# A post-norm decoder layer on one core: inner layer transposed by DMA, its maxima in PSUM, row sums taken with the residual, and new orders on all engines

## The reference

```python
x = _layernorm(x + _L0_attn_ref(x))          # itself x + message; per position l: softmax(q q^T / 8) q over 32 x 64
x = _layernorm(x + _L0_xattn_ref(x, ctx_4096, ctx_4096, ...))
x = _layernorm(x + _L0_ffn_ref(x, ...))

# cross attention, 8 heads of 64, per batch (linear attention):
qh = softmax(Wq x, axis=-2) * SCALE; kh = softmax(Wk ctx, axis=-1); vh = Wv ctx
context = einsum('bhdn,bhen->bhde', kh, vh); out = einsum('bhde,bhdn->bhen', context, qh)
out = Wo out + bo; out / max(|out|, 1e-12) * g * 8

# inner layer, 512 -> 1376 -> 512:
mx_linear(silu(mx_linear(x, w_gate)) * mx_linear(x, w_up), w_down)
# mx_linear quantizes both operands: in each group of 32 along the last axis,
# scale = 2^(floor(log2(max|x|)) - 7), then rounding to an 8-bit float, times scale
```

## Time and profile before

| | us |
|---|---|
| median of 3 runs (725.84 to 727.15) | 726.65 |
| the profiled execution | 726.31 |
| its span in the profile | 724.5 |
| busy in it: PE, DVE, POOL, ACT | 659.2, 601.4, 504.5, 459.7 |
| mean granted TensorE clock, share of full | 0.964 |

### The profile page before, as it was taken

The page is one execution under the profiler, slowest core; times in us unless marked ns, Lnnn a source line. Parts: engine busy times, 40 slices in busy tenths (PEclk is TensorE's granted clock), DMA queues, the critical chain, the costliest instruction groups (busy, mean ns, idle before and its releaser), DMA issues.

```text
span 724.5 us, 14262 instructions
## 1 busy us (share of the span) xinstructions
PE 659.2 (91%) x5392; PEld 361.2 (50%) x5392; DVE 601.4 (83%) x897; ACT 459.7 (63%) x837; POOL 504.5 (70%) x631
## 2 busy tenths in 40 slices
PE   0649898899999999999999999999999989898894
PEld 0649895344454454454554454444545544454451
DVE  2749967997978999998898988888986479989995
ACT  3319574887686787787687787677776523444353
POOL 1512735887888688788878878688777567735785
PEclk9956999999999999999999999999999999999998
DMA  8990002010001010010110110110100000111102
GB/s 311 162 246 8 31 31 67 14 24 0 30 9 31 7 38 29 8 38 1 37 38 1 37 38 2 37 30 4 42 8 12 8 16 16 43 45 52 44 29 88
DMA packets 38916, 31.07 MB, mean 43 GB/s; under 512 B 21184, under 2 KB 29376, under 8 KB 38848
## 3 DMA queue, kind: packets, MB, share of 16 engines
q1 hardware_dynamic: 38848, 30.16, 15.5%
HBM read 21.82 MB, written 4.19 MB: 36 GB/s over the span
## 4 chain that ended last, share of the span: by engine, by line
PE 70%; DVE 13%; issue 7%; POOL 5%; ACT 2%; DMA 2%; SPq 0%; POOLq 0%; DVEq 0%; ACTq 0%
PE banks L2461 9%; PE banks L2471 9%; PE banks L2508 8%; PE banks L2428 8%; PE banks L2438 8%; PE banks L2485 8%; PE banks L2545 5%; PE banks L2413 4%; PE banks L2396 3%; DVE big L876 2%; DMA big<-in_x_dram 2%; PE banks L2523 2%; PE banks L2515 2%; DVE big L881 2%; DVE big L1039 1%
## 5 line engine op out<-in xcount | busy, mean ns | idle before, releaser
L1659 ACT ACTIVATE big<-banks 128x512 f32<-128x512 f32 (+1 forms) x336 | 188.6, 592 | 103.5 <-PE banks L2461 47.7
L548 POOL TENSOR_TENSOR big<-big 128x512 f32<-128x512 f32 x128 | 134.6, 1064 | 10.8 <-DVE big L981 10.8
L1720 ACT ACTIVATE big<-banks,big 128x512 f32<-128x512 f32 x128 | 87.3, 687 | 22.2 <-DVE big L961 22.1
L961 DVE TENSOR_REDUCE big<-banks 128x1 f32<-128x512 f32 x128 | 82.1, 675 | 15.4 <-PE banks L2428 15.4
L540 POOL TENSOR_TENSOR big<-big 128x512 f32<-128x512 f32 x64 | 84.5, 1328 | 11.1 <-ACT big L1725 11.1
L2461 PEld LDWEIGHTS banks<-ident,big 128*128 128x128 f32 x512 | 55.3, 142 | 68.3 <-issue 46.3
L967 DVE TENSOR_REDUCE big<-banks 128x16 f32<-128x1024 f32 x64 | 77.2, 1206 | 14.0 <-PE banks L2438 13.7
L2471 PEld LDWEIGHTS banks<-ident,big 128*128 128x128 f32 x512 | 54.7, 141 | 64.9 <-ACT big L1659 38.6
L2461 PE MATMUL banks<-ident,big 128*128 128x128 f32 x512 | 81.6, 284 | 1.1 <-ACT big L1659 0.9
L972 DVE TENSOR_TENSOR big<-banks,big 128x1024 f32<-128x1024 f32 x64 | 77.8, 1215 | 3.4 <-PE banks L2471 2.1
L2471 PE MATMUL banks<-ident,big 128*128 128x128 f32 x512 | 77.6, 282 | 1.0 <-ACT big L1659 0.7
(11 more groups left out here) (104 smaller groups left out, 1188.9 us busy)
## 6 DMA issues: line engine op xcount, KB each, us to landing
big<-in_x_dram SPq DMA_DIRECT2D x8, 1024.0 KB, 13.9
big<-in_ctx_dram SPq DMA_DIRECT2D x16, 256.0 KB, 3.0
out_dram<-big SPq DMA_DIRECT2D x16, 256.0 KB, 2.1
big<-in_L_ffn_w_down_dram SPq DMA_DIRECT2D x4, 688.0 KB, 10.1
big<-in_L_ffn_w_gate_dram SPq DMA_DIRECT2D x10, 256.0 KB, 2.6
big<-in_L_ffn_w_up_dram SPq DMA_DIRECT2D x10, 256.0 KB, 2.7
wg_area<-in_L_xattn_Wq_dram SPq DMA_DIRECT2D x2, 128.0 KB, 11.1
wg_area<-in_L_xattn_Wk_dram SPq DMA_DIRECT2D x2, 128.0 KB, 6.8
```

What stands on the lines that cost most here:

```text
L548: pool.tensor_tensor(e, e, r, ALU.mult).then_inc(s.p_ready, 1)
L1659: return act.activation(dst, src, ACT.Copy)
L1720: act.activation(EK[:, f % 2, par, i], bank[par], ACT.Exp, bias=kneg[:, par, i:i + 1], accum_out=ksum[:, f % 2, par, i:i + 1]).then_inc(s. ...
```

## The change

Four parts. (1) `transpose_h` moves from TensorE and ACT to SP: two DMA transposes for each tile, of 6 and 5 blocks, straight from `hq` to `hqT`, with their own semaphores; `hq` gets 32 zero columns more, cleared once by POOL. (2) In `scale_hidden` the maxima lie in PSUM (banks 4 and 5, free by then); DVE also computes the scale and keeps it there, and `dequant_hidden` reads it there. (3) `add_down` adds the residual and sums each row in one instruction; POOL makes the mean (`out_mean`), ACT squares the centred row and sums it (`square_out`), and `out_stats` is gone. (4) All orders behind the self-attention are written out anew, call by call, without loops, with a new table for `tr_no`, and SP's queue too.

```diff
+            def transpose_h(u, r):
+                sp.wait_ge(s.hq_ready, u + 1)
+                if u < 2:
+                    sp.wait_ge(s.hq_cleared, 1)
+                else:
+                    sp.wait_ge(s.down_part, 2 * u + r - 3)
+                f0, f1 = ((0, 6), (6, FT))[r]
+                sp.dma_start_transpose(hqT[:, u % 2, f0:f1], hq[:, u % 2, P * f0:P * f1]
+                                       ).then_inc(s.h_transposed[2 * (u % 2) + r], 16)
...
+            def out_mean(u):
+                k = u % 2
+                pool.wait_ge(s.down_added, u + 1)
+                pool.tensor_scalar(neg_mean_o[:, k:k + 1], sum_o[:, k:k + 1], -1.0 / L, None, ALU.mult
+                                   ).then_inc(s.out_mean_ready, 1)
...
-                group_max(hk[u % 2][0], hs[:, u % 4]).then_inc(s.h_inv_ready, 1)
+                else:
+                    dve.wait_ge(s.tr_copied, len(tr_no))
+                amax = bank[4 + u % 2][:, 0:GH]
+                ch.link(dve.tensor_reduce(amax, groups(hs[:, u % 4]), X, ALU.max, apply_absolute_value=True))
+                ch.link(dve.tensor_scalar(hk[u % 2][0].bitcast(I32), amax.bitcast(I32), 0x7F800000, None, ALU.bitwise_and))
+                dve.tensor_scalar(amax, hk[u % 2][0], TINY, 2.0 ** -7, ALU.max, ALU.mult).then_inc(s.h_inv_ready, 1)
...
-                dve.tensor_tensor(groups(hq[:, u % 2]), groups(h8), spread(hk[u % 2][2], GH), ALU.mult
+                dve.tensor_tensor(groups(hq[:, u % 2, 0:FFN]), groups(h8), spread(bank[4 + u % 2][:, 0:GH], GH), ALU.mult
                                   ).then_inc(s.hq_ready, 1)
...
-                dve.tensor_tensor(yo[:, u % 2], xt[:, u], bank[6 + u % 2], ALU.add).then_inc(s.down_added, 1)
-
-            def out_stats(u):
...
+                dve.tensor_tensor_reduce(out=yo[:, u % 2], in0=xt[:, u], in1=bank[6 + u % 2], scale=1.0, scalar=0.0,
+                                         op0=ALU.add, op1=ALU.add, accum_out=sum_o[:, u % 2:u % 2 + 1]
+                                         ).then_inc(s.down_added, 1)
...
+            def square_out(u):
+                k = u % 2
+                act.wait_ge(s.out_mean_ready, u + 1)
...
+                act.activation(spare, yo[:, k], ACT.Square, bias=neg_mean_o[:, k:k + 1],
+                               accum_out=square_o[:, k:k + 1]).then_inc(s.out_squared, 1)
...
             def down(u, r):
-                pe.wait_ge(s.tr_copied, tr_no[u, f"h{r}"] + 1)
+                pe.wait_ge(s.h_transposed[2 * (u % 2) + r], 16 * (u // 2) + 16)
```

More of the change, by code:

```diff
@@ L288, in decoder_kernel @@
         s.hq_ready = sem("hq_ready")
+        s.hq_cleared = sem("hq_cleared")
+        s.h_transposed = [sem(f"h_transposed_{part}") for part in range(4)]
         s.down_part = sem("down_part")
         s.down_added = sem("down_added")
+        s.out_mean_ready = sem("out_mean_ready")
+        s.out_squared = sem("out_squared")
         s.out_ready = sem("out_ready")
@@ L367, in decoder_kernel @@
-        for t, group in middle_groups:
-            tr_no[t, group] = len(tr_no)
-        for u in range(7, 9):
-            for behind, group in turn_groups:
-                if u - behind in tiles:
-                    tr_no[u - behind, group] = len(tr_no)
-        for t, group in last_groups:
-            tr_no[t, group] = len(tr_no)
+        transposed = (
[36 rows of a table added]
+        )
+        tr_no = {group: n for n, group in enumerate(transposed)}
         def aw_group(a):
@@ new lines, in _ @@
+            load_aw(0)
+            load_item(0)
+            load_item(1)
+            load_x(0)
+            load_x(1)
+            load_x(2)
+            load_x(3)
+            load_small()
+            load_xq(0)
+            load_xq(1)
+            load_xq(2)
+            load_xq(3)
+            load_aw(1)
+            load_aw(2)
+            load_item(2)
+            load_aw(3)
+            load_ctx(0)
+            load_ctx(1)
+            transpose_item(0)
+            load_aw(4)
+            load_aw(5)
@@ new lines, in _ @@
+            transpose_h(3, 1)
+            transpose_h(4, 0)
+            transpose_x(9)
+            store(0)
+            transpose_h(4, 1)
+            transpose_h(5, 0)
+            transpose_h(5, 1)
+            store(1)
+            transpose_x(10)
+            store(2)
+            transpose_x(11)
+            transpose_h(6, 0)
+            store(3)
+            transpose_h(6, 1)
+            transpose_h(7, 0)
+            transpose_h(7, 1)
+            transpose_x(12)
+            transpose_x(13)
@@ new lines, in _ @@
+            transpose_h(8, 0)
+            transpose_h(8, 1)
+            store(4)
+            transpose_h(9, 0)
+            transpose_h(9, 1)
+            store(5)
+            transpose_x(14)
+            store(6)
+            transpose_x(15)
+            transpose_h(10, 0)
+            transpose_h(10, 1)
+            transpose_h(11, 0)
+            store(7)
+            transpose_h(11, 1)
+            transpose_h(12, 0)
+            transpose_h(12, 1)
+            transpose_h(13, 0)
+            store(8)
@@ L463, in _ @@
+            store(9)
+            transpose_h(13, 1)
+            store(10)
+            transpose_h(14, 0)
+            transpose_h(14, 1)
+            store(11)
+            transpose_h(15, 0)
+            transpose_h(15, 1)
+            store(12)
+            store(13)
+            store(14)
+            store(15)
             for slot in range(2):
@@ L591, in _ @@
             shift_aw(0)
[L592 removed]
             shift_item(0)
[L594 to L597 removed]
+            for n in range(0, 5):
+                norm_scores(n)
             shift_aw(1)
@@ L2333, in _ @@
+            silu(14, 1)
+            square_out(9)
+            silu(14, 2)
+            result(8)
+            result(9)
+            silu(15, 0)
+            silu(15, 1)
+            silu(15, 2)
+            square_out(10)
+            square_out(11)
+            result(10)
+            result(11)
+            square_out(12)
+            for n in range(13, 16):
+                square_out(n)
+                result(n - 1)
+            result(15)
         @block.tensor
@@ L3038, in _ @@
-            transpose_h(T - 2, 1)
-            down(T - 2, 0)
-            down(T - 2, 1)
-            transpose_h(T - 1, 0)
-            transpose_h(T - 1, 1)
-            down(T - 1, 0)
-            down(T - 1, 1)
+            gate_up(14, 1)
+            gate_up(14, 2)
+            down(10, 0)
+            down(10, 1)
+            gate_up(15, 0)
+            gate_up(15, 1)
+            down(11, 0)
+            down(11, 1)
+            gate_up(15, 2)
+            for n in range(12, 16):
+                down(n, 0)
+                down(n, 1)
```

3263 lines of the change are left out of this document (1858 added, 1405 removed), and 46 rows, old and new, of tables (first_groups, transposed).

## The result

The changed kernel takes 689.96 us (median of 4, 688.46 to 691.75) where the kernel before takes 726.25 in the same series: ratio 0.950, 95% interval 0.947 to 0.953. A second series, on another occasion, gave 0.948 (0.946 to 0.950). The forecast was 692.3, with a range from 680 to 711. The profiled execution took 688.46 us with a span of 686.7, against 726.31 and 724.5.

The account below looks back on a forecast made before the run. TensorE was taken to bound the attention alone, TensorE and DVE together the inner layer. 726.3 - 7.6 (transposes) - 17.9 (attention order) - 9.5 (inner layer) + 1.0 (tail) = 692.3 us, range 680 to 711.

Parts of the forecast that it names:

- h off TensorE: Tiles outside the tail: removing 12.5 transposes of h, 0.61 us each, from TensorE saves 7.6 us.
- the inner layer's loss: Inner layer: 11.45 us of idle TensorE and 2.5 us of lowered clock, 14 us, of which 9.5 come back.
- Order of the attention: Attention: like steps side by side save TensorE 23.9 us; 6 us set aside for late DVE, leaving -17.9.
- The first rival: Attention: DVE and waits for POOL need the 28.0 us slot anyway, so grouping gives nothing; 710.2 us, chance 0.17.
- Maxima in PSUM: Inner layer, DVE: three small operations replace one, 0.16 to 0.18 us for both PSUM ones, costing 0.2 a tile.
- Gives back the 0.38 of L877: Inner layer, DVE: the mask of maxima, 0.560 us on average and 0.184 at best, no longer waits for POOL.
- Sums with the residual: Residual addition on DVE: with the row sum 0.88 us, replacing bn_stats and its aggregate; saves 0.5 to 0.7 a tile.
- I keep a third of the loss: Inner layer: TensorE still waits, with only two pairs of banks for gate-up, so 9.5 of 14 us come back.
- DMA transposes outside the tail: SP's queue: landings of 5 us are hidden by some 28 us of other groups; cost taken as nothing.
- rivals of SP's queue: SP's queue: each transfer must land before the next, 10.8 us a tile against 7.4; 732 us, chance 0.04.
- blocks one by one: DMA transposes: each block crosses singly, 0.58 to 0.8 us each; 707 to 747 us, chance 0.01.
- Tail: After the last dequantization: second DMA piece lands later, -0.2 to +1.6 us, and the norm's hand-overs add 0.3; +1.0 taken.

Follow-up runs that it names:

- e1: The changed kernel with a transpose and the first of two following logits groups swapped at 44 places in the attention: 704.97 us, ratio 0.972 to the kernel before.
- e2: The changed kernel with a transpose and the first of two following a or y products swapped at 27 places: 702.45 us, ratio 0.968 to the kernel before.
- e5: The changed kernel with only maximum and mask in SBUF, the scale still written to and read from PSUM: 690.98 us, ratio 0.950 to the kernel before.
- e6: The changed kernel with only the dequantization changed, reading the scale that POOL wrote to SBUF: 706.34 us, ratio 0.974 to the kernel before.
- e3: The changed kernel with maximum, mask and scale of the inner layer in SBUF again: 703.23 us, ratio 0.970 to the kernel before.
- e4: The changed kernel with the last norm's statistics by bn_stats and aggregate on DVE again, without row sum and squaring: 706.19 us, ratio 0.973 to the kernel before.
- e8: The kernel before with only the transposes of h moved to DMA, all orders but SP's as before: 726.82 us, ratio 1.000 to the kernel before.
- e9: The kernel before with h transposed by DMA and the maxima and scale in PSUM, orders but SP's as before: 723.85 us, ratio 0.996 to the kernel before.
- e11: The changed kernel with two tail additions ahead of the last clip and the last tile done in halves: 689.49 us, ratio 0.947 to the kernel before.

## Why the prediction was right, and where it was not

- **The sum.** 692.3 against 689.96 in the median, 688.46 profiled. By terms, from the stages: slots 14.8 x 1.28 = 18.9 (forecast 17.9), h off TensorE 7.6 (taken over, not measured by itself), the inner layer's loss from 14.9 to 2.6, so 12.3 (9.5), tail +1.7 (+1.0). That gives -37.1 of the span's -37.8; 0.7 lie in the front and in rounding. The loss before was 14.9 and not the prediction's 14: windows of 1 us show a granted clock of 0.50 twice (mean 0.66 from 590 to 595 us, 0.57 from 635 to 639), which costs 3.4 us, where the rounded 0.98 gave 2.5. The first is in the earlier trace rows, behind the wait of 1.99 us for DVE's product: the group from 590.74 to 592.34 takes 1.60 us, where those with 480 columns take 0.81 from 596.85 on.
- **Order of the attention: right, with its mechanism.** e1 and e2 show the price at 82 to 85% of the rows' size with waits and the stretches at a granted clock of 0.50 taken off. TensorE's idle time up to the first gate-up rose by 6.7 us where 6 were set aside; "near 99%" was too much, it is 97.7.
- **The first rival** (DVE holds the attention) didn't come: DVE is busy for 93% of the stretch, and TensorE waits for it for 3.3 us.
- **Maxima in PSUM: priced by the hold-ups of before, which the new order changed.** "Gives back the 0.38 of L877" and "up to 0.17 more" for L1061 are the hold-ups of the old order. In the new one the mask's price is nothing that can be measured (e5), and the dequantization's is 18 us in all (e6): the step that failed is to carry the hold-ups of one order into another. The mean of 1.76 in the earlier trace rows was one tile at 3.77 beside fifteen at 1.59, which shows what the operation cost where it met POOL's scaling (it began at 629.94, inside the scaling from 629.26 to 632.26). The undisturbed sizes were right to 0.04: 0.20, 0.21 and 1.58.
- **Sums with the residual: right in kind, mis-sized.** 0.88 was taken, 0.68 + 0.08 measured: the sum costs nothing beside the addition (0.678 without it), the read 0.08.
- **"I keep a third of the loss": too cautious.** 2.6 of 14.9 are left. But the working behind it, in which DVE's savings simply add up to a reserve, is not how it behaves: undoing either saving costs 15 to 18 us (e3, e4), more than the whole loss. The terms of a sum made one by one held here only because all of them happened. That the total came out within 3 us owes something to luck: no row had shown the 15 to 18 us.
- **DMA transposes outside the tail: right for the new order only.** "The down product stands about four tiles behind" holds there, with one wait of 0.76 us in the tail. In the order of before the same part was worth nothing (e8), so the term of 7.6 isn't one that the transposes carry by themselves. Landing and issue were within their bounds (2.7 us; 1.23 us), and the rivals of SP's queue and of blocks one by one fell.
- **Tail: right in size, wrong in most of its cause.** The norm's +0.3 came (+0.4, from the last down product to the end). The rest isn't the landing but an addition that stands behind the last dequantization, and the granted clock after the pause, 0.50 until 676 us, where before it was 1.00 through the last down product.

## What to carry to other kernels

Before a DVE operation is called slow, look at its longest beside its median: where the longest is close to the sum of its own time and of a POOL operation's (3.89 us by 1.58 and 2.51 in e6), move one of its inputs to PSUM or the operation to another place. In the order of before that took the longest dequantization from 3.77 to 1.59 us, and the four masks of 0.95 to 1.62 us to 0.20 (e9). A hold-up that is rare in one order can be frequent in the next. On a TensorE that never idles, count the changes of kind in its order; like steps side by side were worth 0.15 to 0.20 us for each pair here. And price a part of a change in the order that it will stand in: the maxima in PSUM were worth some 3 us in the order of before (e9 less e8), and 15 when they were taken out of the whole (e3). Last, before two traces are compared by a time late in them, look where they part: a stretch at a granted clock of 0.50 in the attention (345 to 348 us in e11) goes with a first gate-up 2.1 to 2.8 us later here.

## What the runs showed of the hardware

- A DMA transpose has a fixed part and a small one for each block of 128 x 128: 1.19 us of issue and 2.5 to landing with 4 blocks (2.3 in the kernel before), 1.23 and 2.7 with 5 or 6, 1.38 and 3.5 with 11.
- A clip of 768 columns, SBUF to SBUF, took 1.35 us when it began at 672.07 inside POOL's scaling, where one of 608 took 0.47: the one input of the clip didn't keep it clear of POOL, unlike the dequantization with one input in SBUF and one in PSUM.
- TensorE, kept busy with matmuls that nobody reads, kept a granted clock of 1.00 through waits of 0.3 us; with a wait of 2.90 us in their place it had 0.50 from 673 to 679 us, most of the 7.67 us that the last 22 matmuls took.
- A `tensor_tensor` with both inputs in SBUF and POOL's scaling held each other up, whichever came second: the dequantization took up to 3.89 us instead of 1.58, and the scaling up to 3.79 instead of 2.51 (e6). With one input in PSUM neither did in 16 tiles (at most 1.59 and 2.51).
